# Context rows moved from TensorE matmuls to ScalarE copies into the conv banks, and another order of the last tiles, in a convolution and quantised dense kernel

## The chip, the core and the metric

The kernel runs on one core of one Trainium2 chip. The metric is the device time of one execution in microseconds. Times in the profile are counted from the first instruction of the profiled execution.

## What is computed

The input x has 64 samples of 64 channels by 1024 positions. A grouped convolution (4 groups of 16 channels, 9 taps) is taken of x; to each sample and output channel a context value is added, the same for all 1024 positions. Each row of 1024 is then fake-quantised to 8 bits, multiplied by a 1024x1024 weight matrix quantised to 8 bits by column, a 16-bit quantised bias is added, the row is fake-quantised again and added to x:

```python
def _fake_quant(x, bits, axis):
    bound = float(2 ** (bits - 1) - 1)
    absmax = jnp.max(jnp.abs(x), axis=axis, keepdims=True)
    scale = absmax / bound
    ...
    return jnp.round(jnp.clip(x / scale, -bound, bound)) * scale

out = conv1d(x, weight, groups=4)               # (64, 64, 1024), 9 taps
ctx = jnp.einsum('nd,od->no', c, c_weight)      # (64, 64), C_DIM = 128
conv = out + ctx[:, :, None] + bias[None, :, None]
xq = _fake_quant(conv, bits=8, axis=-1)
kq = _fake_quant(kernel, bits=8, axis=0)
y = jnp.einsum('bsd,df->bsf', xq, kq) + _fake_quant(ffn_bias, bits=16, axis=-1)
result = x + _fake_quant(y, bits=8, axis=-1)
```

## The kernel before

The work is cut into 32 tiles; a tile is 8 samples by the 16 output channels of one group, 128 rows of 1024. Tile 31 is LAST, tile 29 is ACT_T. The program is written out by hand for each of the five queues, with semaphores; the order of each queue is the order of the code. A step k of the steady loop handles several tiles at once, and each engine has its own part.

TensorE (L560 on): conv(k) writes tile k into one of two conv banks (conv_ps, 128x1024 each, used by turns). conv_start (L443) waits until the levels of tile k-2 have been rounded out of that bank, adds the context by two matmuls of 128x512 with ctx2 as weights and a repeated selection matrix as moving operand (L449, with start=True, so they overwrite the bank), and then the first four of twelve real matmuls (L436; x and the taps are each split into two fp32r parts, and three of the four products are taken). turn_levels(k-1) (L471) transposes the rounded levels of the tile before into turn_ps. dense(t, h) (L482) is a dense half: 8 bf16 matmuls of 128x512 into one dense bank (L491). spread_max(k) (L463) spreads the column maxima over the rows. Each ordinary step has two dense halves, the first half of tile k-2 and the second half of an older tile (LATE = 5 steps behind at first). At the steps of CATCH_UP an extra second half is done, so that steps 14, 18 and 22 hold three dense halves, and two steps later VectorE has two outputs to measure.

VectorE (L750 on) does in a step: column_max (L652, L660), out_scale, the maximum, scale and reciprocal of the outputs whose turn it is (L702, L690, L693), scale_half of the first half (L638), levels (L670 to L681, the last of them rounds to a_int), add_bias of the first half (L647) and scale_half of the second half (L638).

ScalarE (L397 on): take_levels (L341) copies turn_ps to SBUF as bf16, round_x (L311) makes the first part of x two tiles ahead, quantise (L356, L359) rounds an output and scales it back. GpSimd (L274 on) makes x_lo (L241), adds the bias of second halves (L249) and adds x (L267). The last tiles have forms of their own: tile 29's dense halves are scaled by row on ScalarE (scale_rows, L349) and finished on GpSimd (scale_and_add, L253), and tile 31 is done in halves on VectorE and ScalarE (quantise_last, add_x_last). SyncE issues the loads and stores; x for the final addition is loaded into a ring of six, each load behind the store of an earlier tile in the queue.

In the start (the code up to the steady loop) the dense weights are measured by VectorE (k_levels, L605), rounded by ScalarE (k_round, L316), turned by TensorE (k_turn, L496) and taken by ScalarE (k_take, L325 and L323) in between the first six tiles. The second dense half of tile 0 waits for the last k_take. The context itself is computed at the very start: two matmuls (L421, L423), then two VectorE instructions (L591, L594) that write it as two fp32r parts.

## Time and profile before

| | us |
|---|---|
| median of 3 runs (273.69 to 274.70) | 273.71 |
| the profiled execution | 274.26 |
| its span, first to last instruction | 272.5 |
| TensorE busy (matmul) | 250.8 |
| VectorE busy | 223.1 |
| GpSimd busy | 195.3 |
| ScalarE busy | 157.1 |
| mean granted TensorE clock, share of full speed | 0.973 |

A row of an instruction group names the line, the engine and the operation, then output<-inputs and their shapes, the number of instructions, busy time and mean duration, and the idle time of the engine just before them with what ended it. Matmuls overlap, so a matmul's own duration is longer than the distance between two of them. PE is TensorE, DVE VectorE, ACT ScalarE, POOL GpSimd. In the timeline each row has the start in us, the duration in us (of the whole run of instructions where it says x4), and in brackets how long the engine had been idle and what released it. A busy engine is not by that the bound; where it sits idle, and for whom, has to be read from the timeline.

### The profile page before, as it was taken

To read this page: it belongs to the slowest core of one execution; us is meant where nothing else is said; L and a number is where in the kernel's file an instruction comes from. 1 tells how busy PE (TensorE), PEld (TensorE's weight loads), DVE (VectorE), ACT (ScalarE), POOL (GpSimd) and SP (SyncE) were. 2 spreads that over 40 slices of the span, in tenths; PEclk is the share of its full clock that TensorE was granted. 3 is DMA by queue.
4 is the path that set the end of the run, shared out by engine and by line. 5 is a ranking of instruction groups with operands and counts; after the bars stand their busy time and mean duration, and the time that the engine had idled before them with its cause. 6 is when DMAs were issued, how large, how long until landed. Compare 5 with 4: busy or idle time off the path is not lost.

```text
span 272.5 us, 4059 instructions
## 1 busy us (share of the span) xinstructions
PE 250.8 (92%) x1350; PEld 163.6 (60%) x1372; DVE 223.1 (82%) x446; ACT 157.1 (58%) x156; POOL 195.3 (72%) x105
## 2 busy tenths in 40 slices
PE   7689999899999999999999999999999999999900
PEld 3377666566666666656666666656666666665400
DVE  2696799757888888888898899988899899888853
ACT  5277678523565555665586367735684566645841
POOL 2535433254888888869899798997889888848973
PEclk9979999999999999999999999999999999999965
DMA  6995952340266566764547566584558664444094
GB/s 232 399 409 218 325 216 96 130 155 2 86 214 204 200 227 233 233 232 159 202 181 266 198 234 231 191 267 177 205 182 295 233 231 156 154 155 156 1 363 176
DMA packets 15799, 56.04 MB, mean 206 GB/s; under 512 B 1954, under 2 KB 1954, under 8 KB 15778
## 3 DMA queue, kind: packets, MB, share of 16 engines
q1 hardware_dynamic: 15488, 55.71, 57.6%
q8 instruction: 11, 0.18, 0.3%
q10 hardware_dynamic: 290, 0.07, 0.1%
q14 instruction: 10, 0.08, 0.1%
HBM read 38.99 MB, written 16.78 MB: 205 GB/s over the span
## 4 chain that ended last, share of the span: by engine, by line
PE 76%; DVE 9%; ACT 5%; issue 3%; DMA 3%; POOL 2%; SPq 0%; DVEq 0%; ACTq 0%; POOLq 0%
PE dense_ps L491 34%; PE conv_ps L436 29%; PE conv_ps L449 5%; PE turn_ps L477 4%; DMA k_raw<-ffn_kernel 3%; PE small_ps L467 2%; DVE y_max L702 2%; DVE small_ps L652 2%; DVE k_max L605 2%; ACT k_int L316 2%; ACT kq L325 1%; POOL o_sb L267 1%; PE dense_ps L513 1%; PE turn_ps L504 1%; DVE y L647 1%
## 5 line engine op out<-in xcount | busy, mean ns | idle before, releaser
L491 PE MATMUL dense_ps<-kq,a_t 128*128 128x512 bf16 x474 | 112.8, 379 | 1.9 <-ACT k_scale_b L323 0.6
L241 POOL TENSOR_TENSOR x_lo<-xwin,x_hi 128x1032 fp32r<-128x1032 f32 x32 | 76.8, 2402 | 44.3 <-ACT x_hi L311 38.1
L267 POOL TENSOR_TENSOR o_sb<-y,o_sb 128x1024 f32<-128x1024 f32 x31 | 73.7, 2383 | 20.8 <-ACT y L359 20.8
L491 PEld LDWEIGHTS dense_ps<-kq,a_t 128*128 128x128 bf16 x496 | 47.5, 101 | 46.2 <-issue 1.1
L341 ACT CAST a_t<-turn_ps 128x1024 bf16<-128x1024 int16 x32 | 32.4, 1012 | 66.0 <-PE turn_ps L477 66.0
L652 DVE TENSOR_REDUCE small_ps<-conv_ps 128x8 f32<-128x1024 f32 x32 | 39.4, 1230 | 21.9 <-PE conv_ps L436 21.9
L356 ACT ACTIVATE y_int<-y,y_inv 128x1024 int16<-128x1024 f32 x31 | 35.6, 1147 | 26.9 <-DVE y_inv L693 26.9
L702 DVE TENSOR_REDUCE y_max<-y 128x1 f32<-128x1024 f32 x31 | 37.5, 1210 | 3.1 <-POOL y L249 2.9
L681 DVE TENSOR_TENSOR a_int<-conv_ps,inv 128x1024 int16<-128x1024 f32 x32 | 39.2, 1224 | 0.0
L249 POOL TENSOR_TENSOR y<-y,bq 128x512 f32<-128x512 f32 x30 | 38.1, 1275 | 1.0 <-DVE y L638 1.0
L359 ACT ACTIVATE y<-y_int,y_scale 128x1024 f32<-128x1024 int16 x31 | 35.7, 1152 | 1.0
L436 PE MATMUL conv_ps<-x_hi,w_lo 128*128 128x512 f32 x128 | 35.8, 402 | 0.0
L436 PE MATMUL conv_ps<-x_hi,w_hi 128*128 128x512 f32 x128 | 35.7, 401 | 0.0
L436 PE MATMUL conv_ps<-x_lo,w_hi 128*128 128x512 f32 x128 | 35.3, 398 | 0.0
L311 ACT CAST x_hi<-xwin 128x1032 fp32r<-128x1032 f32 x32 | 33.8, 1056 | 1.6 <-DMA xwin<-x_windows 1.6
L436 PEld LDWEIGHTS conv_ps<-x_lo,w_hi 128*128 128x128 f32 x128 | 24.1, 188 | 6.3 <-POOL x_lo L241 0.3
L436 PEld LDWEIGHTS conv_ps<-x_hi,w_hi 128*128 128x128 f32 x128 | 24.6, 192 | 4.8
L436 PEld LDWEIGHTS conv_ps<-x_hi,w_lo 128*128 128x128 f32 x128 | 23.8, 189 | 5.6
L449 PE MATMUL conv_ps<-select,ctx 128*128 128x512 f32 x64 | 25.2, 477 | 1.1 <-ACT x_hi L311 1.1
L638 DVE SCALAR_TENSOR_TENSOR dense_ps<-dense_ps,row_scale,k_scale_b 128x512 f32<-128x512 f32 x31 | 23.0, 743 | 3.0 <-PE dense_ps L491 2.9
L638 DVE SCALAR_TENSOR_TENSOR y<-dense_ps,row_scale,k_scale_b 128x512 f32<-128x512 f32 x29 | 21.5, 742 | 2.3 <-PE dense_ps L491 2.3
L647 DVE TENSOR_TENSOR y<-dense_ps,bq 128x512 f32<-128x512 f32 x31 | 21.1, 680 | 0.1
(69 smaller groups left out, 190.7 us busy)
## 6 DMA issues: line engine op xcount, KB each, us to landing
xwin<-x_windows SPq DMA_DIRECT2D x32, 516.0 KB, 4.4
o_sb<-x_rows SPq DMA_DIRECT2D x32, 512.0 KB, 4.5
out<-o_sb SPq DMA_DIRECT2D x31, 512.0 KB, 2.9
k_raw<-ffn_kernel SPq DMA_DIRECT2D x4, 1024.0 KB, 12.5
w_raw<-taps SPq DMA_DIRECT2D x2, 256.0 KB, 3.1
b_row<-ffn_bias SPq DMA_DIRECT2D x1, 512.0 KB, 12.8
out<-o_sb SPq DMA_DIRECT2D x2, 256.0 KB, 2.7
condt<-cond_t ACTq DMA_DIRECT2D x1, 32.0 KB
```

Source lines behind the costliest of these rows:

```text
L241: pool.tensor_tensor(x_lo[:, at].rearrange("p n b -> p (n b)"), xwin[:, t % XWIN, :], x_hi[:, at].bitcast(F32).rearrange("p n b -> p (n b) ...
L249: pool.tensor_tensor(y[:, t % YRING, half(h)], y[:, t % YRING, half(h)], bq[:, half(h)], ALU.add).then_inc(s["biased1"], 1)
L267: pool.tensor_tensor(o_sb[:, at, :], y[:, t % YRING, :], o_sb[:, at, :], ALU.add).then_inc(s["o_made"], 1)
L356: act.activation(y_int[:, t % 2], y[:, t % YRING, :], ACT.Copy, scale=y_inv[:, t % 2:t % 2 + 1]).then_inc(s["y_rounded"], 1)
L359: act.activation(y[:, t % YRING, :], y_int[:, t % 2], ACT.Copy, scale=y_scale[:, t % 2:t % 2 + 1]).then_inc(s["y_dequantised"], 1)
L436: mm = pe.matmul(conv_ps[:, at, hs, :].rearrange("p (n b) -> p n b", n=NH), w[:, ch, g].rearrange("p q o -> p (q o)"), x[:, x_at, hs * NH: ...
L449: pe.matmul(conv_ps[:, at, hs, :].rearrange("p (n b) -> p n b", n=NH), ctx2[:, g].rearrange("k q o -> k (q o)"), select[:, ns].unsqueeze(2 ...
L491: mm = pe.matmul(dense_bank(t, h), a_t[:, t % LEVELS, q].rearrange("b j o -> b (j o)"), kq[:, q, half(h)], start=(q == 0), stop=(q == Q - 1))
L638: dve.scalar_tensor_tensor(out=to, in0=dense_bank(t, h), scalar=row_scale[:, t % RSRING:t % RSRING + 1], in1=k_scale_b[:, half(h)], op0=AL ...
L652: dve.tensor_reduce(cmax_ps, conv_ps[:, t % 2].rearrange("p h (n b) -> p (h n) b", b=BLOCKS), AX_X, ALU.max, apply_absolute_value=True).th ...
L681: dve.tensor_tensor(a_int[:, at, :].rearrange("p (n b) -> p n b", b=BLOCKS), conv_cols(at), inv8[:, at].unsqueeze(2).to_broadcast([P, NS, ...
L702: dve.tensor_reduce(y_max[:, at], y[:, t % YRING, :], AX_X, ALU.max, apply_absolute_value=True).then_inc(s["y_max_made"], 1)
```

## The change

The context is no longer added by matmuls. At the start TensorE computes it as one column per sample for each group (8 small matmuls, from weights that VectorE repeats first), VectorE copies it to ctx_cols, and ScalarE writes it, repeated over the 128 positions of a block, into the conv bank of each tile (seed, a new function; L315 of the changed kernel). The real matmuls then add to what the bank holds. conv_start waits for that copy. The two-part context, the selection matrix and cond2 go. warm_up, the matmuls that keep TensorE busy at the start, now writes into the conv banks.

In the two-output steps VectorE measures the second output after the levels and at the end of the step. In step 31 all outputs come after the levels. ScalarE takes both halves of tile 29 one after the other and quantises tile 27 a step later. The bias of tile 30's second half is added by VectorE and not by GpSimd.

```diff
         def pool_adds(t, h):
-            return h == 1 and t < LAST and t != ACT_T
+            return h == 1 and t < LAST - 1 and t != ACT_T
...
+        def ctx_bank(g):
+            return small_ps[:, 0:N] if g == 0 else turn_f32[:, (g - 1) * N:g * N]
...
+            def seed(t):
+
+
+                g, n0 = t % GROUPS, t // GROUPS * NS
+                wait(act, "ctx_made", 1 if g == 0 else 2)
+                wait(act, "a_rounded", t - 1)
+                act.copy(conv_cols(t % 2), ctx_cols[:, g, n0:n0 + NS].unsqueeze(2)
+                         .to_broadcast([P, NS, BLOCKS])).then_inc(s["seeded"], 1)
...
+            seed(0)
             round_x(0)
+            seed(1)
             k_round(0)
             k_round(1)
...
             k_take(5)
+            seed(5)
             take_levels(3)
...
             k_take(7)
+            seed(6)
             take_levels(4)
             k_take(8)
             k_take(9)
             round_x(7)
             for k in range(6, second_step(LAST) + 2):
+                if there(k + 1):
+                    seed(k + 1)
                 if there(k - 1):
                     take_levels(k - 1)
                 if there(k + 2):
                     round_x(k + 2)
                 if k == LAST:
-                    scale_rows(ACT_T, 0)
-                for t in outs(k):
-                    quantise(t)
-                if k == LAST:
-                    scale_rows(ACT_T, 1)
+                    for h in range(2):
+                        scale_rows(ACT_T, h)
+                else:
+                    for t in (outs(LAST) if k == LAST + 1 else []) + outs(k):
+                        quantise(t)
             quantise_last()
...
-            def warm_up():
-                for i in range(WARM):
-                    pe.matmul(turn_f32.rearrange("p (i f) -> p i f", f=P), ident[:],
+            def warm_up(at):
+                for hs in range(2):
+                    pe.matmul(conv_ps[:, at, hs, :].rearrange("p (i f) -> p i f", f=P), ident[:],
                               ident[:].unsqueeze(1).to_broadcast([P, JH, P]),
                               start=True, stop=True)
 
+            def context(g):
+                pe.matmul(ctx_bank(g), cwt_q[:, g].rearrange("d q o -> d (q o)"),
+                          condt[:], start=True, stop=False)
+                return pe.matmul(ctx_bank(g), cbias_q[:, g].rearrange("d q o -> d (q o)"),
+                                 ones[0:1, 0:N], start=False, stop=True)
+
             pe.wait_ge(s["ident_made"], 1)
-            warm_up()
-            pe.wait_ge(s["cond_made"], 1)
-            pe.matmul(small_ps[:, 0:C], cond2[:].rearrange("d p n -> d (p n)"), cwt[:],
-                      start=True, stop=False)
-            pe.matmul(small_ps[:, 0:C], ones[0:1, :], cbias[:], start=False, stop=True
-                      ).then_inc(s["ctx_mm"], 1)
-            warm_up()
+            warm_up(0)
+            pe.wait_ge(s["cond_in"], 48)
+            pe.wait_ge(s["cond_made"], 2)
+            context(0).then_inc(s["ctx_mm"], 1)
+            warm_up(1)
+            pe.wait_ge(s["cond_made"], 4)
+            for g in range(1, GROUPS):
+                mm = context(g)
+            mm.then_inc(s["ctx_mm"], 1)
...
             def conv_start(t):
-                at, g, n0 = t % 2, t % GROUPS, t // GROUPS * NS
-                wait(pe, "a_rounded", t - 1)
+                wait(pe, "seeded", t + 1)
                 wait(pe, "hi_made", t + 1)
-                for hs in range(2):
-                    ns = slice(n0 + hs * NH, n0 + (hs + 1) * NH)
-                    pe.matmul(
-                        conv_ps[:, at, hs, :].rearrange("p (n b) -> p n b", n=NH),
-                        ctx2[:, g].rearrange("k q o -> k (q o)"),
-                        select[:, ns].unsqueeze(2).to_broadcast([P, NH, BLOCKS]),
-                        start=True, stop=False, skip_group_check=True)
                 terms(t, ((x_hi, w_hi),))
...
+            dve.wait_ge(s["cond_in"], 48)
+            for gs in (slice(0, 1), slice(1, GROUPS)):
+                for to, row in ((cwt_q, cwt), (cbias_q, cbias)):
+                    dve.tensor_copy(to[:, gs], row[:, gs.start * CG:gs.stop * CG]
+                                    .rearrange("d (g o) -> d g o", o=CG).unsqueeze(2)
+                                    .to_broadcast([to.shape[0], gs.stop - gs.start, Q, CG])
+                                    ).then_inc(s["cond_made"], 1)
             dve.wait_ge(s["ctx_mm"], 1)
-            dve.tensor_copy(ctx_r[:], small_ps[:, 0:C]).then_inc(s["ctx_rounded"], 1)
-            dve.wait_ge(s["ctx_rounded"], 1)
-            dve.tensor_copy(ctx2[0:N], ctx_r[0:N].bitcast(F32).rearrange("k (g o) -> k g o", g=GROUPS)
-                            .unsqueeze(2).to_broadcast([N, GROUPS, Q, CG])
-                            ).then_inc(s["ctx_made"], 1)
-            dve.tensor_tensor(
-                ctx2[N:P],
-                small_ps[N:P, 0:C].rearrange("k (g o) -> k g o", g=GROUPS)
-                .unsqueeze(2).to_broadcast([N, GROUPS, Q, CG]),
-                ctx_r[N:P].bitcast(F32).rearrange("k (g o) -> k g o", g=GROUPS)
-                .unsqueeze(2).to_broadcast([N, GROUPS, Q, CG]), ALU.subtract
-                ).then_inc(s["ctx_made"], 1)
+            dve.tensor_copy(ctx_cols[:, 0], ctx_bank(0)).then_inc(s["ctx_made"], 1)
+            dve.wait_ge(s["ctx_mm"], 2)
+            dve.tensor_copy(ctx_cols[:, 1:GROUPS].rearrange("p g n -> p (g n)"),
+                            turn_f32[:, 0:(GROUPS - 1) * N]).then_inc(s["ctx_made"], 1)
...
                     wait(dve, "biased0", but_act(t))
-                    wait(dve, "biased1", but_act(t))
+                    if t < LAST - 1:
+                        wait(dve, "biased1", but_act(t))
+                    else:
+                        dve.wait_ge(s["biased_last"], 1)
...
@@ -752,18 +766,20 @@
                 column_max(k)
                 if len(again) == 2:
                     scale_half(again[0], 1)
-                for t in outs(k):
-                    out_scale(t)
                 if k < LAST:
+                    for t in outs(k)[:1]:
+                        out_scale(t)
                     scale_half(k - LAG, 0)
                 levels(k)
                 if k < LAST:
                     add_bias(k - LAG, 0)
                     scale_half(again[-1], 1)
+                for t in outs(k)[k < LAST:]:
+                    out_scale(t)
             out_scale(LAST - 3)
-            scale_half(LAST - 1, 0)
-            add_bias(LAST - 1, 0)
-            scale_half(LAST - 1, 1)
+            for h in range(2):
+                scale_half(LAST - 1, h)
+                add_bias(LAST - 1, h)
             out_scale(LAST - 2)
             scale_half(LAST, 0)
             add_bias(LAST, 0)
```

In ScalarE's queue, in the start, where the last four blocks of the dense weights are rounded and taken (k_int, kq, k_scale_b). Before:

```order
L316 ACTIVATE k_int<-k_raw,k_inv 128x1024 x2
L325 CAST kq<-dense_ps 128x8x128
L341 CAST a_t<-turn_ps 128x8x8x16
L325 CAST kq<-dense_ps 128x8x128
L323 COPY k_scale_b<-dense_ps 128x512
L311 CAST x_hi<-xwin 128x1032
```

and in the changed kernel:

```order
L320 ACTIVATE k_int<-k_raw,k_inv 128x1024 x2
L329 CAST kq<-dense_ps 128x8x128
L315 COPY conv_ps<-ctx_cols 128x1024
L345 CAST a_t<-turn_ps 128x8x8x16
L329 CAST kq<-dense_ps 128x8x128
L327 COPY k_scale_b<-dense_ps 128x512
L306 CAST x_hi<-xwin 128x1032
L315 COPY conv_ps<-ctx_cols 128x1024
```

Two copies into conv_ps have come in: one between the two kq copies (for tile 6), and one behind x_hi (for tile 7).

ScalarE's queue in two ordinary steps of the steady loop. Before:

```order
L356 ACTIVATE y_int<-y,y_inv 128x1024
L359 ACTIVATE y<-y_int,y_scale 128x1024
L341 CAST a_t<-turn_ps 128x8x8x16
L311 CAST x_hi<-xwin 128x1032
L356 ACTIVATE y_int<-y,y_inv 128x1024
L359 ACTIVATE y<-y_int,y_scale 128x1024
L341 CAST a_t<-turn_ps 128x8x8x16
```

and in the changed kernel:

```order
L360 ACTIVATE y_int<-y,y_inv 128x1024
L363 ACTIVATE y<-y_int,y_scale 128x1024
L315 COPY conv_ps<-ctx_cols 128x1024
L345 CAST a_t<-turn_ps 128x8x8x16
L306 CAST x_hi<-xwin 128x1032
L360 ACTIVATE y_int<-y,y_inv 128x1024
L363 ACTIVATE y<-y_int,y_scale 128x1024
L315 COPY conv_ps<-ctx_cols 128x1024
```

The copy into the conv bank stands between the output's two passes and the levels' copy out of turn_ps.

VectorE's queue near the end, from the first half of tile 30 (held in conv_ps) to the first half of tile 31 (in dense_ps). Before:

```order
L638 SCALAR_TENSOR_TENSOR conv_ps<-conv_ps,row_scale,k_scale_b 128x512
L647 TENSOR_TENSOR y<-conv_ps,bq 128x512
L638 SCALAR_TENSOR_TENSOR y<-conv_ps,row_scale,k_scale_b 128x512
L702 TENSOR_REDUCE y_max<-y 128x1
L690 TENSOR_SCALAR y_scale<-y_max 128x1
L693 RECIPROCAL y_inv<-y_scale 128x1
L638 SCALAR_TENSOR_TENSOR dense_ps<-dense_ps,row_scale,k_scale_b 128x512
```

and in the changed kernel:

```order
L649 SCALAR_TENSOR_TENSOR conv_ps<-conv_ps,row_scale,k_scale_b 128x512
L658 TENSOR_TENSOR y<-conv_ps,bq 128x512
L649 SCALAR_TENSOR_TENSOR conv_ps<-conv_ps,row_scale,k_scale_b 128x512
L658 TENSOR_TENSOR y<-conv_ps,bq 128x512
L716 TENSOR_REDUCE y_max<-y 128x1
L701 TENSOR_SCALAR y_scale<-y_max 128x1
L704 RECIPROCAL y_inv<-y_scale 128x1
L649 SCALAR_TENSOR_TENSOR dense_ps<-dense_ps,row_scale,k_scale_b 128x512
```

The second half of tile 30 is now scaled within the bank and gets its bias here; before it was scaled into y, for GpSimd to add the bias.

## Rows read from the trace of the kernel before

**Rows 1.** The page, parts 1 and 4: busy time of each engine, and the chain.

```profile
PE 250.8 (92%) x1350; PEld 163.6 (60%) x1372; DVE 223.1 (82%) x446; ACT 157.1 (58%) x156; POOL 195.3 (72%) x105
...
PE 76%; DVE 9%; ACT 5%; issue 3%; DMA 3%; POOL 2%; SPq 0%; DVEq 0%; ACTq 0%; POOLq 0%
```

**Rows 2.** Timeline of an ordinary step: start, duration, engine, line, operation, idle before.

```profile
228.84 0.78 PE L449 MATMUL conv_ps<-select,ctx 128*128 128x512 f32 x2
...
229.46 1.11 PE L436 MATMUL conv_ps<-x_hi,w_hi 128*128 128x512 f32 x4
...
232.48 1.23 DVE L652 TENSOR_REDUCE small_ps<-conv_ps 128x8 f32<-128x1024 f32 x1 [0.79 <-PE conv_ps L436]
...
232.95 1.01 ACT L341 CAST a_t<-turn_ps 128x1024 bf16<-128x1024 int16 x1 [2.43 <-PE turn_ps L477]
...
239.83 1.23 DVE L652 TENSOR_REDUCE small_ps<-conv_ps 128x8 f32<-128x1024 f32 x1 [0.81 <-PE conv_ps L436]
```

**Rows 3.** Groups of instructions by line: context matmuls and two ScalarE groups.

```profile
L359 ACT ACTIVATE y<-y_int,y_scale 128x1024 f32<-128x1024 int16 x31 | 35.7, 1152 | 1.0
...
L311 ACT CAST x_hi<-xwin 128x1032 fp32r<-128x1032 f32 x32 | 33.8, 1056 | 1.6 <-DMA xwin<-x_windows 1.6
...
L449 PE MATMUL conv_ps<-select,ctx 128*128 128x512 f32 x64 | 25.2, 477 | 1.1 <-ACT x_hi L311 1.1
```

**Rows 4.** Timeline: first matmuls of tiles 6 and 31.

```profile
53.58 0.78 PE L449 MATMUL conv_ps<-select,ctx 128*128 128x512 f32 x2
...
243.53 0.78 PE L449 MATMUL conv_ps<-select,ctx 128*128 128x512 f32 x2
```

**Rows 5.** The chain late in the run: start, us, engine, tile, line, count.

```profile
236.53 0.43 PE conv_ps L449 x2
236.96 2.83 PE conv_ps L436 x12
...
242.15 1.73 PE dense_ps L491 x8
```

**Rows 6.** Timeline of step 24, with two outputs, and the spread of tile 25.

```profile
195.17 1.23 DVE L652 TENSOR_REDUCE small_ps<-conv_ps 128x8 f32<-128x1024 f32 x1 [0.81 <-PE conv_ps L436]
...
196.87 1.22 DVE L702 TENSOR_REDUCE y_max<-y 128x1 f32<-128x1024 f32 x1 [0.21 <-issue]
...
203.46 1.22 DVE L652 TENSOR_REDUCE small_ps<-conv_ps 128x8 f32<-128x1024 f32 x1
...
204.99 0.30 PEld L467 LDWEIGHTS small_ps<-col_max,same_b 128*128 128x128 f32 x2 [0.57 <-DVE col_max L660]
```

**Rows 7.** Timeline of the start: VectorE at tile 3, ScalarE with the last weights.

```profile
33.35 1.22 DVE L652 TENSOR_REDUCE small_ps<-conv_ps 128x8 f32<-128x1024 f32 x1
...
44.57 2.19 ACT L316 ACTIVATE k_int<-k_raw,k_inv 128x1024 int16<-128x1024 f32 x2 [1.08 <-DVE k_inv L612]
...
48.78 1.03 ACT L325 CAST kq<-dense_ps 128x1024 bf16<-128x1024 int16 x1
...
51.31 0.59 ACT L323 COPY k_scale_b<-dense_ps 128x512 f32<-128x512 f32 x1 [1.50 <-PE dense_ps L504]
```

**Rows 8.** Timeline of the end.

```profile
247.18 1.23 DVE L652 TENSOR_REDUCE small_ps<-conv_ps 128x8 f32<-128x1024 f32 x1 [0.80 <-PE conv_ps L436]
...
249.16 0.33 PE L467 MATMUL small_ps<-col_max,same_b 128*128 128x64 f32 x2
...
255.16 0.75 DVE L638 SCALAR_TENSOR_TENSOR y<-conv_ps,row_scale,k_scale_b 128x512 f32<-128x512 f32 x1 [0.46 <-PE conv_ps L491]
...
261.76 1.22 DVE L702 TENSOR_REDUCE y_max<-y 128x1 f32<-128x1024 f32 x1 [2.92 <-POOL y L249]
...
266.47 0.16 DVE L693 RECIPROCAL y_inv<-y_scale 128x1 f32<-128x1 f32 x1
```

**Rows 9.** The page, part 2, TensorE's clock, and a timeline row of the start.

```profile
PEclk9979999999999999999999999999999999999965
...
14.17 0.62 PE L513 MATMUL dense_ps<-ident_b,k_int 128*128 128x128 bf16 x8 [1.73 <-ACT k_int L316]
```

More of the change, by code:

```diff
@@ L34 @@
 DVE_K = (2, 3)
-WARM = 2
 LAST = TILES - 1
@@ L58, in build @@
         warm = sb("warm", [P, 2], F32)
-        select = sb("select", [P, N], F32R)
         w_raw = sb("w_raw", [P, 2, Q, GROUPS, CG], F32)
@@ L63, in build @@
         condt = sb("condt", [C_DIM, N], F32)
-        cond2 = sb("cond2", [C_DIM, 2, N], F32)
         cwt = sb("cwt", [C_DIM, C], F32)
         cbias = sb("cbias", [1, C], F32)
-        ctx_r = sb("ctx_r", [P, C], F32R)
-        ctx2 = sb("ctx2", [P, GROUPS, Q, CG], F32R)
+        cwt_q = sb("cwt_q", [C_DIM, GROUPS, Q, CG], F32)
+        cbias_q = sb("cbias_q", [1, GROUPS, Q, CG], F32)
+        ctx_cols = sb("ctx_cols", [P, GROUPS, N], F32)
         k_raw = sb("k_raw", [P, KB, Q * P], F32)
@@ L108, in build @@
             "cond_in", "b_in", "ones_made", "ident_made", "ident_b_made", "warm_made",
-            "mask_made", "mask_q_made", "same_made", "same_b_made", "select_made", "cond_made", "ctx_mm",
-            "ctx_rounded", "ctx_made", "w_hi_made", "w_lo_made",
+            "mask_made", "mask_q_made", "same_made", "same_b_made", "cond_made", "ctx_mm",
+            "ctx_made", "seeded", "w_hi_made", "w_lo_made",
             "k_max_made", "k_scale_made", "k_inv_made", "k_rounded_dve", "k_rounded_act",
@@ L295, in _ @@
             act.copy(ident_b[:], ident[:]).then_inc(s["ident_b_made"], 1)
-            for part in range(2):
-                rows = slice(part * N, (part + 1) * N)
-                act.copy(select[rows, :], ident[rows, rows]).then_inc(s["select_made"], 1)
-            act.wait_ge(s["cond_in"], 48)
-            act.copy(cond2[:], condt[:].unsqueeze(1).to_broadcast([C_DIM, 2, N])
-                     ).then_inc(s["cond_made"], 1)
             for ch in range(2):
@@ L376, in _ @@
             round_x(2)
+            seed(2)
             take_levels(0)
             round_x(3)
+            seed(3)
             take_levels(1)
@@ L381, in _ @@
             bias_levels()
+            seed(4)
             take_levels(2)
@@ L518, in _ @@
             pe.wait_ge(s["ident_b_made"], 1)
-            pe.wait_ge(s["select_made"], 2)
             pe.wait_ge(s["ctx_made"], 2)
@@ L717, in maximum_last @@
             def maximum_last(h):
-                wait(dve, "biased_last" if h else "biased0", 1 if h else but_act(LAST))
+                wait(dve, "biased_last" if h else "biased0", 2 if h else but_act(LAST))
                 dve.tensor_reduce(last_max[:, h:h + 1], y[:, LAST % YRING, half(h)], AX_X, ALU.max,
```

## Prediction

> **What bounds the kernel now.** I read the page first. TensorE is busy for 92% of the span and carries 76% of the chain that ended last; VectorE is at 82%, GpSimd at 72%, ScalarE at 58% [rows 1]. Then the timeline of one ordinary step late in the run [rows 2]. A step lasts 7.35 us (two column maxima, 232.48 and 239.83), and TensorE does not stop in it. VectorE sat idle 0.80 us of it, just before its column maximum, so its own work in a step is 7.35 - 0.80 = 6.55 us. ScalarE sat idle 2.43 us before it took the turned levels. So TensorE sets the step, VectorE stands 0.80 us behind it, and ScalarE has a hole. Of the time on TensorE the 64 context matmuls (L449) are the only group that can go without touching the real work [rows 3].
>
> Steps of this kind run from tile 6 (53.58) to tile 31 (243.53), 25 of them in 189.95 us [rows 4]. 25 x 7.345 is 183.6; three steps hold one more dense half, 8 matmuls in 1.73 us [rows 5], together 5.2. The remaining 1.2 us are stalls behind the three steps in which VectorE has two outputs to measure.
>
> **The change, part by part.** *Context matmuls out of each step.* The chain gives the two of them 0.43 us and the twelve real conv matmuls 2.83 us, 0.236 each [rows 5]; the timeline puts 0.62 us from the first context matmul (228.84) to the first real one (229.46) [rows 2]. The extra 0.15 over 2 x 0.236 = 0.47 belongs to the first fp32 matmul behind a bf16 one, and the first real conv matmul now stands there. I take 0.47 and keep 0.43 and 0.62 as ends. The step becomes 7.345 - 0.47 = 6.875 us, still above VectorE's 6.55. 25 steps: **-11.75 us** (ends -10.75 and -15.5).
>
> *A ScalarE copy of 128x1024 into the conv bank in each step.* No row shows ScalarE writing PSUM. The nearest is the x_hi copy, 1.056 us for 1032 elements [rows 3]; I take 1.1 us, with 1.0 and 1.5 as ends. It is queued behind the output's two passes and ahead of the copy of the turned levels, and that is where the hole of 2.43 us lies [rows 2]. With 0.47 less per step the hole is 1.96, so the copy fits at either end. The bank is free when VectorE has rounded tile k, before the middle of step k+1's convolution, and it is wanted a step later. What ScalarE had to do was 1.01 + 1.06 + 2 x 1.15 = 4.4 us a step [rows 2, 3]; 5.5 us now, under 6.875. Cost in an ordinary step: nothing. If the cover went, it would cost what it exceeds the hole by.
>
> *The steps with two outputs.* There VectorE needs 8.29 us (195.17 to 203.46), 0.2 of it a pause [rows 6], thus 8.1. It starts the next column maximum 8.1 - 6.875 = 1.2 us late, where here it was 8.29 - 7.345 = 0.95. TensorE wants the maximum only after the turn and one dense half: the spread matmul followed the column maximum by 1.53 us where it waited (203.46 to 204.99) [rows 6] and by 1.99 where it did not, so 0.45 us is free. Stall 0.75 us (ends 0.5 and 1.0). The second output now comes at the end of VectorE's step, so its two ScalarE passes start late too, and the context copy for tile k+2 is queued behind them: by my times it ends about 0.2 us after TensorE wants it. Together some 0.9 us each, 2.7 against 1.2 before: **+1.5 us** (ends +0.3 and +2.4). VectorE makes up 0.32 us a step, so the lag does not spread.
>
> *The start.* Here ScalarE is the queue that matters. Up to tile 5 the missing matmuls bring TensorE forward by about 0.9 us. The context is made a little later (four small VectorE copies, eight small matmuls), but tile 0's convolution has slack until the first rounded weights. VectorE's run of work from the column maximum at 33.35 on moves only 0.4 us, since the bias levels come 0.3 us later out of ScalarE behind two context copies. So k_int starts at 44.2 in place of 44.57 [rows 7]. From there ScalarE is on the path: k_int x2, kq, context copy of tile 6, levels, kq (before: ending 48.78 + 1.03 = 49.81). With a copy of 1.1 more, and 0.5 gained, the last ends at 50.4; the last scales, 51.31 before, come at 51.9; the dense half behind them frees TensorE for tile 6 at 54.2. Before, the context matmul began at 53.58 and the first real one 0.62 later, 54.2 too [rows 4, 7]. Gain up to tile 6: **0** (ends -0.6 and +0.8, by copies of 1.0 and 1.5 us).
>
> The Trainium skill ("VectorE: DVE Perf Modes", the errata table of op costs) gives a ScalarE instruction that reads SBUF 224 cycles and one per element, by which an estimate for this copy is (224 + 1024)/1.2 GHz = 1.04 us. It says too ("ScalarE: Activation LUTs", what happens in an ACTIVATE) that writing PSUM is quicker than writing SBUF. By 1.04 for 1.1 the start, with two copies on its path, would be 0.1 us shorter. No row here shows it.
>
> *The end.* VectorE's queue from the column maximum of tile 31 (247.18) to the last reciprocal (266.47) [rows 8] changes four ways. The wait for GpSimd's bias of tile 30, 2.92 us at 261.76, goes. VectorE does that bias itself, +0.70 (as its others). The levels of tile 31 come before the output of tile 27, and must wait for the spread matmul (249.16 and about 0.37 to its use), from about 248.65 (1.47 behind the start of the column maximum) to 249.53: +0.87. In exchange VectorE is busy when the second half of tile 30 is ready, so its wait of 0.46 at 255.16 goes. Sum -2.92 + 0.70 + 0.87 - 0.46 = -1.8. ScalarE takes tile 29's second half directly, and GpSimd runs its four final adds, 2.35 each, by 266.4 in place of 268.15; the last stores follow. Tile 31's x is loaded behind tile 28's store, which GpSimd now finishes about a microsecond later, and may hold the last additions by 0 to 0.7. I take **-1.5 us** (ends -0.7 and -1.9).
>
> **Sum.** -11.75 + 1.5 + 0 - 1.5 = -11.75 us. The profiled execution took 274.26 us, its span 272.5. So the span should be 260.8 and that execution 262.5. It stood 0.55 above the median of 273.71, so I forecast **262.0 us**. With the best end of each term it would be 256.0, with the worst 265.8.
>
> **Rivals.** *The switch penalty goes with the context matmuls.* Then a step loses 0.62 and is 6.725 us, still over 6.55. 25 x 0.15 = 3.8 us more: 258.2. For it: the chain's rows give the penalty no place. Against: the first weight load behind a bf16 one stays. Chance 0.12.
>
> *VectorE becomes the bound.* Its margin is 0.32 us a step. ScalarE's write into one PSUM bank runs beside VectorE's bias (0.68) and second scaling (0.74) in others. If these slow by 0.3 each, VectorE needs 7.15 a step, TensorE waits 0.27, 25 times: 6.8 us back, about 269. Against it: the column maximum lasts 1.23 us while ScalarE reads PSUM beside it (232.48 and 232.95) [rows 2], as it does on average. Chance 0.11.
>
> *TensorE's clock falls in the start.* The page shows it at 0.7 in one slice, around the pause that ended at 14.17 [rows 9]. That pause grows by half a microsecond, and a new one of about 1.2 us opens before tile 2, whose context copy waits in ScalarE's queue. At the lower level (1.2 GHz) the 4 us of matmuls behind it would take 8, about 2 of which would reach tile 6: 264. The Trainium skill ("TensorE: Matmul & The Clock Gate", the HAM clock gate) says that idling brings the array to half clock and sustained work releases it; that speaks against this change, and for this rival. Chance 0.06.
>
> *ScalarE becomes the bound, and the kernel slower.* Its step is 4.4 us plus the copy. From a copy of 2.5 us on it exceeds TensorE's 6.875, from 2.95 the old 7.345. At 3.2 a step takes 7.6: 25 x 0.26 = +6.5, the start loses about 4, the end gives 1.5: 283. For it: a copy with a repeated innermost element into PSUM, which no ScalarE row shows. Against: all its copies here of some 1024 elements take 1.01 to 1.16 us, whatever their strides and types. Chance 0.03. Between this and the forecast lies a copy that misses its slot often, with little gain left: 272 to 273, chance 0.03.
>
> **How the numbers follow.** Forecast 0.65, rivals 0.12, 0.11, 0.06, 0.03 and 0.03. The forecast's own range is 260 to 264.5. For 8 in 10 I reach down to the first rival and up to a second one of 0.25 us for each of the two instructions (step 7.05, 266.4): 258.0 to 267.0. Half a per cent, 1.4 us, is about what a measurement of this kernel tells from no change. Faster by more: all but the last two, 0.95. Same 0.02, slower 0.03.
>
> **What would show it.** Ordinary steps of 6.87 us (6.72 for the first rival, 7.1 for the second); a copy of 1.0 to 1.15 us into conv_ps, followed by a wait for turn_ps of still about 0.9; VectorE's idle time before the column maximum down from 0.80 to about 0.3; tile 6 starting near 54.2; three steps longer by up to a microsecond behind two outputs; no wait of VectorE for GpSimd near the end, and some 23.7 us from the last tile's column maximum to the end, against 25.3 (247.18 to 272.5). I am wrong if the ordinary step is not shorter, or if the wait for the copy (L315 before a conv matmul) stands in every step.

## The result, and the profile after

The changed kernel takes **266.81 us** (median of 4 runs, 265.76 to 268.01) against 273.7 (273.0 to 274.7) for the kernel before in the same comparison: ratio 0.976, 95% interval 0.9733 to 0.9787. That is 6.9 us faster where 11.7 were forecast. The profiled execution took 268.01 us with a span of 265.1 (before 274.26 and 272.5; forecast span 260.8).

The page of the changed kernel: busy times, TensorE's clock in 40 slices, and the chain, to be read against [rows 1, 9].

```profile
PE 240.3 (91%) x1298; PEld 153.2 (58%) x1320; DVE 225.2 (85%) x450; ACT 186.9 (71%) x185; POOL 193.4 (73%) x104
...
PEclk9779999999999999999999999999999999999965
...
PE 65%; DVE 18%; issue 4%; ACT 4%; POOL 4%; DMA 3%; DVEq 0%; ACTq 0%; SPq 0%; POOLq 0%
```

TensorE lost 10.5 us of work, ScalarE took on 29.8. The chain moved from TensorE (76% to 65%) to VectorE (9% to 18%), and the clock line has a second slice at 7 near the start: both point at the ends of the program, not at the steady steps.

Timeline of an ordinary step, as [rows 2]: start, duration, engine, line, operation, idle before and what ended it.

```profile
157.77 1.29 PE L457 MATMUL conv_ps<-x_hi,w_hi 128*128 128x512 f32 x4
...
159.46 1.02 ACT L315 COPY conv_ps<-ctx_cols 128x1024 f32<-128x1024 f32 x1
...
160.98 1.23 DVE L663 TENSOR_REDUCE small_ps<-conv_ps 128x8 f32<-128x1024 f32 x1 [0.35 <-PE conv_ps L457]
161.45 1.01 ACT L345 CAST a_t<-turn_ps 128x1024 bf16<-128x1024 int16 x1 [0.97 <-PE turn_ps L490]
...
164.68 1.29 PE L457 MATMUL conv_ps<-x_hi,w_hi 128*128 128x512 f32 x4
```

The step is 164.68 - 157.77 = **6.91 us** (7.35 before, 6.875 forecast). VectorE still waits for TensorE before its column maximum, 0.35 us in place of 0.80, and ScalarE's hole shrank from 2.43 to 0.97 us with the copy of 1.02 in it. The four first real matmuls last 1.29 us in place of 1.11 [rows 2]: the surcharge for the first fp32 matmul behind a bf16 one moved onto them.

Two groups by line, as [rows 3]:

```profile
L457 PE MATMUL conv_ps<-x_hi,w_hi 128*128 128x512 f32 x128 | 41.1, 443 | 1.5 <-ACT conv_ps L315 1.0 <-issue 0.5
...
L315 ACT COPY conv_ps<-ctx_cols 128x1024 f32<-128x1024 f32 x32 | 32.4, 1013 | 11.3 <-DVE a_int L692 4.1 <-DVE ctx_cols L610 3.7 <-DVE ctx_cols L608 3.2
```

Over all 32 tiles TensorE waits 1.0 us for the copy. Of the 11.3 us that ScalarE idles ahead of its copies, 6.9 are the first two, in the start.

**Where the time went.** Two marks, the first real conv matmul of tile 6 and of tile 31, cut the span in three. Before, they stand at 54.20 (53.58 + 0.62, [rows 2, 4]) and 244.15:

| us | before | forecast | after |
|---|---|---|---|
| start to tile 6 | 54.2 | 54.2 | 56.88 |
| tile 6 to tile 31 | 189.95 | 179.7 | 180.00 |
| tile 31 to the end | 28.35 | 26.85 | 28.2 |
| span | 272.5 | 260.8 | 265.1 |

The middle came within 0.3 us of the forecast. The start lost 2.7 us that the forecast gave no price, and the end gave 0.15 in place of 1.5.

The start of the changed kernel, TensorE, VectorE and GpSimd (an fp32 matmul stands as two in such a row, so a warm-up pair as x4, one context matmul as x2):

```profile
1.42 3.59 PE L427 MATMUL conv_ps<-ident 128*128 128x512 f32 x4 [1.42 <-POOL ident L227]
4.66 2.47 POOL L233 TENSOR_TENSOR w_lo<-w_raw,w_hi 128x512 fp32r<-128x512 f32 x2 [3.29 <-ACT w_hi L299]
4.75 1.26 DVE L603 COPY cwt_q<-cwt 128x128 f32<-128x128 f32 x1 [2.53 <-DMA cbias<-cond_bias]
5.93 1.28 DVE L603 COPY cbias_q<-cbias 1x128 f32<-1x128 f32 x1
7.14 0.53 DVE L603 COPY cwt_q<-cwt 128x384 f32<-128x384 f32 x1
...
7.36 0.41 PE L432 MATMUL small_ps<-condt,cwt_q 128*128 128x64 f32 x2 [2.35 <-DVE cbias_q L603]
...
8.05 3.68 PE L427 MATMUL conv_ps<-ident 128*128 128x512 f32 x4
...
13.75 0.36 DVE L610 COPY ctx_cols<-turn_ps 128x192 f32<-128x192 f32 x1 [5.36 <-PE turn_ps L434]
14.03 2.27 DVE L616 TENSOR_REDUCE k_max<-k_raw 128x2 f32<-128x2048 f32 x1
```

The same places before, where the context matmuls follow the first warm-up pair at once, the second pair takes 1.98 us, and VectorE's first k_max waits for its load alone:

```profile
5.10 0.59 PE L421 MATMUL small_ps<-cwt,cond 128*128 128x64 f32 x2
...
5.98 1.98 PE L414 MATMUL turn_ps<-ident 128*128 128x512 f32 x4
...
10.20 2.29 DVE L605 TENSOR_REDUCE k_max<-k_raw 128x2 f32<-128x2048 f32 x1 [2.29 <-DMA k_raw<-ffn_kernel]
```

The measuring of the dense weights, and with it everything up to tile 6, begins with this k_max. It now stands in VectorE's queue behind the wait for the last context matmul, and starts at 14.03 in place of 10.20. From there to tile 6 it is 42.85 us, in this execution and in those of a0, e1, e2, e4, e5, e9 and e10 below (42.84 to 42.86): in this kernel tile 6 moves with k_max. Before it was 44.0 (54.20 - 10.20). Three things made that matmul late. The pair stands ahead of the last six context matmuls. The pair took 3.68 us in place of 1.98, with the granted clock at 0.52 from 8 to 11 us, the level of 1.2 GHz. And two small VectorE copies of 128 columns lasted 1.26 and 1.28 us (the one of 384 columns 0.53), so TensorE stood 2.35 us before the context. Whether that pause made the pair slow is not shown: in e3 below, the same pair took 3.78 us with no pause ahead of it.

The end, as [rows 8]:

```profile
254.77 0.43 SPq L199 DMA_DIRECT2D o_sb<-x_rows  x1
...
257.52 0.16 DVE L704 RECIPROCAL y_inv<-y_scale 128x1 f32<-128x1 f32 x1
...
260.73 1.41 DVE L725 SCALAR_TENSOR_TENSOR o_sb<-y_int,y_scale,o_sb 128x512 f32<-128x512 int16 x2 [3.05 <-DMA o_sb<-x_rows]
```

VectorE reaches the last reciprocal 20.64 us behind tile 31's mark; before it was 266.47 - 244.15 = 22.32. The new order gave its 1.7 us. Then VectorE waits 3.05 us for the x of tile 31, issued at 254.77 and landed 5.9 us later. Before, VectorE's wait was for ScalarE only:

```profile
260.86 0.43 SPq L198 DMA_DIRECT2D o_sb<-x_rows  x1
...
267.49 1.86 DVE L711 SCALAR_TENSOR_TENSOR o_sb<-y_int,y_scale,o_sb 128x512 f32<-128x512 int16 x2 [0.86 <-ACT y_int L367]
```

The load is issued 17.9 us behind tile 31's mark in place of 16.7, the add is due 1.7 us sooner. The DMA view of this one load, before (window 260.5 to 261.5) and after (254.5 to 255.5), gives its size and the us from issue to landing:

```profile
o_sb<-x_rows SPq DMA_DIRECT2D x1, 512.0 KB, 4.5
...
o_sb<-x_rows SPq DMA_DIRECT2D x1, 512.0 KB, 5.9
```

So of its 6.63 us from issue to use before, 4.5 were needed and 2.1 were to spare. The new places of load and add take 2.9 of them, 0.8 too many, and the landing itself took 1.4 us longer: together the 2.2 us by which the wait of 3.05 exceeds ScalarE's 0.86.

### The profile page after: what moved, and what is told of

The parts are those of the page before. It is cut to its first block, busy times and chain, and to the rows that moved or that the text cites. A ratio compares the mean times of both kernels' runs of the same rounds, so it can differ in the third digit from the quotient of the medians.

```text
span 265.1 us, 4018 instructions
## 1 busy us (share of the span) xinstructions
PE 240.3 (91%) x1298; PEld 153.2 (58%) x1320; DVE 225.2 (85%) x450; ACT 186.9 (71%) x185; POOL 193.4 (73%) x104
## 4 chain that ended last, share of the span: by engine, by line
PE 65%; DVE 18%; issue 4%; ACT 4%; POOL 4%; DMA 3%; DVEq 0%; ACTq 0%; SPq 0%; POOLq 0%
PE dense_ps L504 30%; PE conv_ps L457 26%; DVE small_ps L663 4%; PE turn_ps L490 4%; DVE k_max L616 3%; DVE y_max L716 3%; DMA o_sb<-x_rows 2%; PE small_ps L480 2%; POOL o_sb L268 2%; PE conv_ps L427 1%; ACT kq L329 1%; DMA cbias<-cond_bias 1%; DVE y L658 1%; DVE dense_ps L649 1%; POOL y L261 1%
## 5 line engine op out<-in xcount | busy, mean ns | idle before, releaser
L663 DVE TENSOR_REDUCE small_ps<-conv_ps 128x8 f32<-128x1024 f32 x32 | 39.3, 1230 | 10.9 <-PE conv_ps L457 10.9
L457 PE MATMUL conv_ps<-x_hi,w_hi 128*128 128x512 f32 x128 | 41.1, 443 | 1.5 <-ACT conv_ps L315 1.0
L315 ACT COPY conv_ps<-ctx_cols 128x1024 f32<-128x1024 f32 x32 | 32.4, 1013 | 11.3 <-DVE a_int L692 4.1
L250 POOL TENSOR_TENSOR y<-y,bq 128x512 f32<-128x512 f32 x29 | 37.0, 1280 | 1.0 <-DVE y L649 1.0
L457 PE MATMUL conv_ps<-x_hi,w_lo 128*128 128x512 f32 x128 | 36.6, 408 | 0.0
L457 PEld LDWEIGHTS conv_ps<-x_hi,w_hi 128*128 128x128 f32 x128 | 23.8, 189 | 9.0 <-ACT conv_ps L315 1.8
```

Of the source, the lines that this page charges most:

```text
L250: pool.tensor_tensor(y[:, t % YRING, half(h)], y[:, t % YRING, half(h)], bq[:, half(h)], ALU.add).then_inc(s["biased1"], 1)
L457: mm = pe.matmul(conv_ps[:, at, hs, :].rearrange("p (n b) -> p n b", n=NH), w[:, ch, g].rearrange("p q o -> p (q o)"), x[:, x_at, hs * NH: ...
L663: dve.tensor_reduce(cmax_ps, conv_ps[:, t % 2].rearrange("p h (n b) -> p (h n) b", b=BLOCKS), AX_X, ALU.max, apply_absolute_value=True).th ...
```

## The experiments

The theory: the middle is as forecast; the start lost 2.7 us because the K-side (the measuring and rounding of the dense weights) queues behind a context that a half-clock warm-up pair and two held copies delay; the end lost 1.5 us to one load in SyncE's queue. The rivals: chance of load landings, the switch of the matmuls itself, or the new order of outputs. Each row gives the median (its range, runs), the 95% interval of the ratio to the kernel before on the same chip (e5's runs lie too far apart for one), and the three parts of the profiled execution.

| | us | ratio, 95% | to tile 6 | 6 to 31 | 31 to end |
|---|---|---|---|---|---|
| a0: the changed kernel again | 264.75 (263.17-265.77, 4) | 0.9617-0.9702 | 56.16 | 179.99 | 26.65 |
| e1: x loads early | 267.28 (265.91-268.4, 4) | 0.9702-0.9779 | 58.89 | 179.96 | 26.65 |
| e2: warm-up first | 264.16 (263.73-265.05, 4) | 0.9618-0.9676 | 53.60 | 180.01 | 28.1 |
| e6: e2, copies by ScalarE | 264.33 (264.21-264.49, 4) | 0.9627-0.9672 | 53.88 | 180.02 | 28.2 |
| e3: before, new order alone | 271.95 (270.73-273.68, 10) | 0.9921-0.9983 | 52.10 | 189.85 | 28.05 |
| e4: after, old order | 267.34 (264.76-269.61, 4) | 0.9671-0.9807 | 56.88 | 180.02 | 28.6 |
| e5: second outputs early | 267.16 (262.69-269.12, 4) | none | 58.92 | 180.02 | 27.6 |
| e9: e1 and e2 | 262.25 (262.15-262.27, 4) | 0.9544-0.9623 | 53.62 | 179.98 | 26.7 |
| e10: e9, copy in the middle | 263.03 (262.25-263.1, 4) | 0.9593-0.9648 | 53.72 | 180.00 | 26.7 |
| e11: e9, tile 6's copy late | 261.57 (261.2-261.64, 4) | 0.9539-0.9587 | 52.94 | 180.03 | 26.6 |
| e12: e10 and e11 | 261.61 (261.34-262.5, 4) | 0.9544-0.9602 | 52.93 | 180.02 | 26.65 |

The spans of all executions tell more than four medians. Those of the changed kernel are 263.6 to 265.1 us in the first comparison and 260.7 to 263.1 in a0; those of e9 are 260.3 four times, of e10 260.3 to 260.6, of e11 259.5 to 259.8, of e12 259.6 to 260.0.

**The changed kernel again (a0).** No edit.

> The changed kernel again, beside which the others of this call are read. About 266.8 us; tile 6's first matmul near 56.9, ordinary steps 6.91, the last additions waiting about 3 us for tile 31's x.

It took 264.75 us here, 2 less than in the first comparison, and the trace says why such runs differ. In this execution cwt_q started before GpSimd's w_lo, and lasted 0.23 us:

```profile
4.59 0.23 DVE L603 COPY cwt_q<-cwt 128x128 f32<-128x128 f32 x1 [2.36 <-DMA cbias<-cond_bias]
4.73 1.28 DVE L603 COPY cbias_q<-cbias 1x128 f32<-1x128 f32 x1
...
13.03 0.36 DVE L610 COPY ctx_cols<-turn_ps 128x192 f32<-128x192 f32 x1 [5.34 <-PE turn_ps L434]
...
258.54 1.41 DVE L725 SCALAR_TENSOR_TENSOR o_sb<-y_int,y_scale,o_sb 128x512 f32<-128x512 int16 x2 [1.58 <-DMA o_sb<-x_rows]
```

The first context matmul came 1.2 us sooner (6.15 against 7.36), but it and the next took 0.5 us more, so the context was done 0.72 us sooner, and tile 6 came 0.72 sooner. The second warm-up pair took 3.66 us. The x load landed 4.5 us after its issue, so the wait was 1.58, 0.7 more than for ScalarE, and the end took 26.65 us. In a third execution of the same start (e1, below) the context was done at 15.78. The changed kernel's start therefore varies by 2.7 us and its end by 1.5, and the middle by 0.04. One execution of a0 that has no trace had a span of 260.7 us, the forecast's 260.8: the changed kernel reaches it by chance.

**x loads early (e1).** The loads of x for tiles 30 and 31 are issued right behind tile 29's:

```diff
-                if there(k - 3):
-                    load_x(k - 3)
+                for t in {LAST + 1: (LAST - 2, LAST - 1, LAST)}.get(k, (k - 3,)):
+                    if there(t) and k <= LAST + 1:
+                        load_x(t)
```

> The changed kernel with the loads of x for tiles 30 and 31 issued right behind that of tile 29, ahead of the stores of tiles 27 and 28. Theory (the end's gain was eaten by tile 31's x, issued at 254.77 and landed at 260.70): the 3.05 us wait of VectorE goes, the span falls by 2.2 to 3 us. Rival (the burst of five stores sets the end whoever is first): the wait goes but the last stores land as late as before, under 0.7 us.

The wait for the load is gone; the add waits 0.86 us for ScalarE, as before:

```profile
260.51 1.87 DVE L726 SCALAR_TENSOR_TENSOR o_sb<-y_int,y_scale,o_sb 128x512 f32<-128x512 int16 x2 [0.86 <-ACT y_int L372]
```

Tile 31 to the end takes 26.65 in place of 28.2 us. The two adds take 1.87 us in place of 1.41, as they run beside GpSimd's last add again, and that gives part of the wait back. The whole was no faster (267.28 against a0's 264.75), where 2.2 to 3 us less were expected. In the start of the profiled execution the context matmuls, too, ran at the slow pace (0.69 us each against 0.43), and ctx_cols came at 15.78. The 26.65 alone proves little, as a0 has it without the edit; with the edit it is 26.6 to 26.7 in all five executions profiled (e9 to e12 below), and without it, in this order, 28.2, 28.1, 28.2 (e6), 27.6 (e5) and once 26.65.

**Warm-up first (e2).**

```diff
             warm_up(0)
+            warm_up(1)
             pe.wait_ge(s["cond_in"], 48)
             pe.wait_ge(s["cond_made"], 2)
             context(0).then_inc(s["ctx_mm"], 1)
-            warm_up(1)
```

> The changed kernel with both warm-up pairs of matmuls ahead of the context matmuls, so that the contexts of groups 1 to 3 no longer stand behind a warm-up pair. Theory (VectorE's first k_max is queued behind its wait for the last context, 14.03 against 10.20 before): k_max starts near 10.6 to 11, tile 6 starts 2 to 2.7 us earlier, 264.3 us. Rival (ScalarE's copies in the weight section hold tile 6): k_max starts earlier but tile 6 gains under 1 us.

```profile
1.42 5.31 PE L427 MATMUL conv_ps<-ident 128*128 128x512 f32 x8 [1.42 <-POOL ident L227]
...
7.37 0.41 PE L432 MATMUL small_ps<-condt,cwt_q 128*128 128x64 f32 x2 [0.64 <-DVE cbias_q L603]
...
10.48 0.36 DVE L610 COPY ctx_cols<-turn_ps 128x192 f32<-128x192 f32 x1 [2.08 <-PE turn_ps L434]
10.76 2.28 DVE L616 TENSOR_REDUCE k_max<-k_raw 128x2 f32<-128x2048 f32 x1
```

Both pairs together take 5.31 us, where one took 3.59 and the other 3.68. They fill the time in which the context's weights are not there, TensorE pauses 0.64 us in place of 2.35, and k_max starts at 10.76. Tile 6 moves from 56.88 (a0: 56.16) to 53.60: the start's loss, and 0.6 us more, is the position of the second pair. The end has its x wait again (2.97 us), and so the whole is only 0.6 us below a0, whose profiled end was a quick one, with intervals that overlap: this gain is read from the traces, and in the time only in e9.

**The small copies by ScalarE (e6, on top of e2).** ScalarE makes cwt_q and cbias_q; VectorE's four copies are deleted.

> As the one before, and the four copies that repeat the context weights are made by ScalarE in place of VectorE. Two of them lasted 1.26 and 1.28 us on VectorE for 128 elements, both ending as a GpSimd instruction ended; a copy of three times the size lasted 0.53. Theory (VectorE was held while GpSimd ran): on ScalarE they last 0.2 to 0.5 us each and the context matmuls start 1 to 1.5 us earlier; k_max starts at 10.2, bound by its load, tile 6 starts about 0.4 us ahead of the kernel before it. Rival (such a copy is slow by its broadcast): they last over 1 us on ScalarE too.

```profile
4.67 0.30 ACT L300 COPY cwt_q<-cwt 128x128 f32<-128x128 f32 x1 [0.59 <-DMA cbias<-cond_bias]
4.87 0.29 ACT L300 COPY cbias_q<-cbias 1x128 f32<-1x128 f32 x1
...
10.78 2.29 DVE L616 TENSOR_REDUCE k_max<-k_raw 128x2 f32<-128x2048 f32 x1 [0.35 <-DMA k_raw<-ffn_kernel]
```

On ScalarE the same copies take 0.30 and 0.29 us, so it is not the repeated input that makes them slow (nor is it in a0, 0.23 us on VectorE). Yet nothing is gained: the context matmuls start at 7.17, behind warm-up pairs that take 5.91 us here, and k_max waits for its load, so with the warm-up first the context is off the path. How much VectorE's two copies of 1.3 us cost with the pair behind them no run shows alone; a0, where the first of them was short, came 0.7 us sooner to tile 6.

**The new order alone (e3)**, on the kernel before: the context by matmuls, all the rest of the change kept.

> The kernel before with the new order alone (second outputs late, last levels first, bias of tile 30 by VectorE), the context still by matmuls. Theory (the end gains 1.7 us up to the last reciprocal and gives most of it back to the late load of x): from tile 31's first real matmul to the end 28.2 or so in place of 28.35, the three steps behind two outputs unchanged within 0.3 us, the time within 0.7 us of before. Rival (the order gains in itself and lost its gain only beside the context copies): 1.5 us faster or more.

The steps stay at 7.34 us. Tile 31 to the end is 28.05 against 28.35, with an x wait of 3.1 us: the order alone brings 0.3. By its ratio (0.9921 to 0.9983) it is 1.3 us below before. In the profiled one tile 6 came 2.1 us early: the first load of the dense weights landed early (k_max at 9.01, 1.2 us sooner), and from 16 to 19 us the granted clock is 1.00 here and 0.50 in the kernel before. How much of the 1.3 is such luck, over 10 runs, stays open. The start of this kernel is that of the kernel before, and its second warm-up pair took:

```profile
6.44 3.78 PE L414 MATMUL turn_ps<-ident 128*128 128x512 f32 x4
```

It had no pause ahead of it, and took as long as the slow pairs of the changed kernel.

**The context copies alone (e4)**, with the old order of outputs and tail.

> The changed kernel with the old order of outputs and of the end: the context copies alone. Theory: ordinary steps of 6.91 us, the steps behind two outputs about 0.6 to 0.8 longer, the end 28.3, thus 0 to 0.5 us slower than the changed kernel; all of the gain is the context's. Rival (the new order is needed for it): over 1.5 us slower than the changed kernel.

It has the same start (56.88) and middle, and VectorE waits 2.93 us for GpSimd's bias again. It agrees with e3: the middle's gain is all the context's, and by these single executions the order is worth 0.3 to 0.4 us as long as the x load stands where it does.

**Both outputs measured early (e5).**

```diff
-                    for t in outs(k)[:1]:
+                    for t in outs(k):
...
-                for t in outs(k)[k < LAST:]:
-                    out_scale(t)
+                if k == LAST:
+                    for t in outs(k):
+                        out_scale(t)
```

> The changed kernel with both outputs measured early in the three two-output steps, the end as changed. Theory (VectorE's work in the step, 8.0 us against 6.91, makes the stall, wherever the second output stands; 0.2 of it is the context copy queued behind the late output): steps behind them 7.5 to 7.7 in place of 7.69. Rival (the late place is what keeps the stall small): 8.0 or more.

The tile behind a two-output step comes after 7.63, 7.62 and 7.63 us in place of 7.69 three times, and the middle still takes 180.02. The late place of the second output brings nothing, and costs nothing. The time of the whole spreads over 6 us with the start (the profiled one had ctx_cols at 15.79) and says nothing here.

**Both repairs (e9)**: the edits of e1 and e2.

> The changed kernel with both edits that mend what my forecast missed: warm-up pairs ahead of the contexts, and the last loads of x early. Theory (the two losses are apart and add): tile 6 near 53.6, 26.6 us from tile 31's first matmul to the end, span 260.2, 262.5 us. Rival (one hides the other): 263.5 or more.

```profile
238.16 1.70 SPq L199 DMA_DIRECT2D o_sb<-x_rows  x3
...
254.24 0.16 DVE L705 RECIPROCAL y_inv<-y_scale 128x1 f32<-128x1 f32 x1
...
255.26 1.87 DVE L726 SCALAR_TENSOR_TENSOR o_sb<-y_int,y_scale,o_sb 128x512 f32<-128x512 int16 x2 [0.86 <-ACT y_int L372]
```

The gains add: 262.25 us, span 260.3 in all four runs, below every span of the changed kernel (eight, from 260.7 to 265.1), and the scatter is gone. The number is near the 262.0 forecast for the change itself, which the changed kernel comes to only at the lucky end of its scatter.

**The copy between two outputs (e10).** In the two-output steps the second output's passes move behind the context copy:

```diff
+                if k <= LAST:
+                    for t in outs(k - 1)[1:]:
+                        quantise(t)
...
-                    for t in (outs(LAST) if k == LAST + 1 else []) + outs(k):
+                    for t in (outs(LAST) if k == LAST + 1 else []) + (outs(k)[:1] if k < LAST else outs(k)):
```

> Both repairs (all warm-up pairs ahead of the contexts, x loads of the last two tiles ahead of two stores), and in the three steps with two outputs ScalarE makes the copy of the context between its passes for the two outputs instead of behind both. Theory (the copy lands late behind two outputs' work, and the convolution waits 0.2 us for it): the tile after a two-output step starts 7.45 to 7.5 us after it instead of 7.69, and the whole takes 261.6 us, 0.6 below the version with both repairs alone (262.25). Rival (what these steps lose is VectorE's own lateness with two outputs to round): followers stay at 7.65 to 7.7 and the time at 262.2.

The theory fell. In the changed kernel the convolution does wait for the copy:

```profile
168.96 1.21 DVE L663 TENSOR_REDUCE small_ps<-conv_ps 128x8 f32<-128x1024 f32 x1
...
170.48 0.30 PEld L480 LDWEIGHTS small_ps<-col_max,same_b 128*128 128x128 f32 x2 [0.95 <-DVE col_max L671]
...
171.31 1.00 ACT L315 COPY conv_ps<-ctx_cols 128x1024 f32<-128x1024 f32 x1
...
172.37 0.77 PEld L457 LDWEIGHTS conv_ps<-x_hi,w_hi 128*128 128x128 f32 x4 [0.21 <-ACT conv_ps L315]
```

The same place in e10:

```profile
163.49 1.02 ACT L316 COPY conv_ps<-ctx_cols 128x1024 f32<-128x1024 f32 x1 [0.29 <-issue]
...
167.33 0.30 PEld L484 LDWEIGHTS small_ps<-col_max,same_b 128*128 128x128 f32 x2 [0.95 <-DVE col_max L675]
...
169.12 0.87 PEld L461 LDWEIGHTS conv_ps<-x_hi,w_hi 128*128 128x128 f32 x4
```

The copy is made 5.6 us ahead of the conv's weight load, and the wait of 0.21 is gone. But the followers come after 7.62 us in place of 7.69, the tiles behind them after 8.62 in place of 8.56, and tile 6 to 31 takes 180.00. What these steps lose is set by VectorE's late column maximum, for which TensorE's spread matmul waits 0.95 us in both.

**Tile 6's copy late (e11).**

```diff
-            seed(6)
             take_levels(4)
             k_take(8)
             k_take(9)
+            seed(6)
             round_x(7)
```

> Both repairs, and the first copy of a context (tile 6's) stands behind ScalarE's last step of the K-side instead of ahead of it. Theory (ScalarE's queue is what tile 6 waits on in the start, so its copy of 1.0 us lies on that path): the work of tile 6 begins at about 52.6 us instead of 53.6, and the whole takes 261.3 us. Rival (the bank's contents are needed by tile 6's convolution at the same moment anyway): tile 6 stays at 53.6 and the time at 262.2.

ScalarE in the start of e11:

```profile
47.36 1.01 ACT L346 CAST a_t<-turn_ps 128x1024 bf16<-128x1024 int16 x1
48.27 1.02 ACT L330 CAST kq<-dense_ps 128x1024 bf16<-128x1024 int16 x1
50.67 0.59 ACT L328 COPY k_scale_b<-dense_ps 128x512 f32<-128x512 f32 x1 [1.39 <-PE dense_ps L518]
51.16 1.02 ACT L316 COPY conv_ps<-ctx_cols 128x1024 f32<-128x1024 f32 x1
...
52.94 1.29 PE L458 MATMUL conv_ps<-x_hi,w_hi 128*128 128x512 f32 x4
```

k_scale_b, which frees the first dense halves, begins at 50.67 in place of 51.36, and tile 6 at 52.94 in place of 53.62: 0.7 us of the 1.0 expected. The last kq ends 0.8 us sooner (49.29 against 50.11 in e9), and k_scale_b behind it then waits 1.39 us for TensorE in place of 1.25. At 261.57 us (0.9539 to 0.9587) this is the best version here, 11.7 us under the kernel before (273.25 on the same chip).

**Both of these (e12).**

> Both repairs, the copy between the two outputs' passes, and tile 6's copy behind the K-side. Theory: the two gains lie in different stretches and add, 260.7 us (262.25 - 0.6 - 1.0), with the pace of ordinary steps at 6.91 us. Rival (neither copy is on the path that sets the end): 262.2 us, the same as with the repairs alone.

261.61 us, as e11: the copy's place among two outputs is worth nothing in either setting.

## Why the prediction was right in direction and short in size

The forecast was 262.0 us in 258.0 to 267.0; it came out at 266.81 in its own comparison, and by its ratio (0.976 of the 273.71 us of the section on the kernel before) at 267.1, just outside.

- **Ordinary steps (-11.75): right, slightly over-sized.** 25 steps at 6.91 us in place of 6.875, so -10.9. The price of two context matmuls is 0.44 us, nearly the 0.43 that the chain gave them, not 0.47. The copy lasts 1.013 us (taken 1.1), sits in ScalarE's hole, and no wait for it stands in an ordinary step. The first rival (the surcharge goes) fell by the 1.29 us of the four first matmuls; the second (VectorE the bound) by VectorE's 0.35 us of idle time.
- **Two-output steps (+1.5): the loss came, smaller.** 0.78 us each (7.69 - 6.91), 0.7 by the time the next step is over, against 0.9; three times 0.7 against 1.2 before is +0.9. Of its two causes only VectorE's lateness counts: e10 took the late copy away for nothing. That the middle as a whole came within 0.3 us is in part luck: this miss and the one above, 0.6 and 0.85, have opposite signs.
- **The start (0, ends -0.6 and +0.8): the step that failed.** It said that "tile 0's convolution has slack until the first rounded weights" and priced the context's new route at nothing. The convolution was not the one to ask: VectorE's k_max stands behind its wait for the last context in the queue, and the K-side from there to tile 6 is the path. The wait that the change adds was not followed to what is queued behind it. It cost 2.7 us in the profiled execution (1.96 in a0, 4.7 in e1), and e2 removed it. The third rival named TensorE's clock in the start, and the half level did come, but it looked for the cost at the pauses by 14 us and before tile 2 instead of at the warm-up pair ahead of k_max. There the half level cost, as an estimate from the pair's 3.68 and 1.98 us, 1.7 us of the 3.8 by which k_max was late.
- **ScalarE's queue in the start: half right.** The copy of tile 6 is on the path, 0.7 us of it (e11). With k_max back in its place the term's sum holds: k_int starts at 44.25 in e9 (forecast 44.2), tile 6 at 53.62 (54.2, end -0.6).
- **The end (-1.5, ends -0.7 and -1.9): mis-sized by the load.** The sum on VectorE's queue, -1.8, measured -1.7. The load of tile 31's x, for which 0 to 0.7 us was left, held the adds by 3.05 us where ScalarE alone would have held them 0.86, 1.55 us by the end of the span. The forecast saw that the load would be issued a microsecond later (1.2), but read no landing time. Before, it had 2.1 us to spare, and 1.2 + 1.7 were taken from it: 0.8 short, about the 0.7 of the forecast's bad end. That is what a0 shows, at no cost to the end (26.65, a gain of 1.7). The rest is the landing, 5.9 us in place of 4.5. It was slow (5.4 to 6.0 us) in e2, e3, e5 and e6 too; why is not shown.
- **Two slips in the sums.** The worst ends add up to 265.5 us, not 265.8, and all chances but the last two to 0.94, not 0.95. Neither bears on the miss.

The sum of the misses: 2.7 + 0.3 + 1.35, about 4.3 us of span, 260.8 to 265.1.

## What to carry to other kernels

When a change puts a new wait into an engine's queue, price it by the first long instruction queued behind it, not by the one that needs the data: here a wait for six tiny matmuls held up the measuring of all weights. When a chain is shortened, look at what the loads beside it had to spare, from issue to landing against issue to use, before counting the gain, and at how far the landing of the same load scatters. Filler that warms TensorE belongs where it would idle anyway, ahead of the awaited work and not between its parts; and a kernel whose runs scatter has a place where chance decides: mending the two of them here took the spread of the span from 4.4 us (eight executions) to 0.4 at most in each of e9 to e12.

## What the runs showed of the hardware

- **Two small VectorE copies ended with GpSimd's instructions.** cwt_q and cbias_q (fp32, SBUF to SBUF) took 1.26 and 1.28 us, ending at 6.01 and 7.21, while GpSimd's two w_lo instructions ran from 4.66 to 7.13. Begun 0.08 us ahead of GpSimd, cwt_q took 0.23 (a0), and on ScalarE 0.30 (e6). The Trainium skill ("SBUF — State Buffer", the section on the two separate sides) says that GpSimd and a VectorE instruction in a mode with two ports (by that page an fp32 copy within SBUF is one) take a shared port pair as an exclusive lock, for the whole instruction, whoever starts first; these rows agree with it.
- **TensorE's pace in the first microseconds can differ where the instructions are the same.** The first context matmuls of the changed kernel took 0.41 us in its first profile and 0.66 in a0. The second warm-up pair took 1.98 us in the kernel before and 3.78 in e3, whose start is the same; in the changed kernel it took 3.68, 3.66 (a0) and 3.78 us (e1) behind pauses of 2.35, 0.95 and 2.15 us. No run shows what decides it. The records of the granted clock do not always show the slow pace: 0.52 from 8 to 11 us after the change, but 1.00 in the same stretch of a0 and e3. The durations are the better witness here.
- **ScalarE writes PSUM with a repeated input at 1.013 us for 128x1024**, 0.04 less than its copy of 1032 elements into SBUF (1.055).
- **The same load lands after 4.5 or 5.9 us** in the last microseconds of the program (a0 and the first profile of the same kernel; 4.5 in the kernel before, 6.0 in e3).
